# Layer norm over a GNN residual: a zero-filled accumulator, and x added on VectorE

## The reference, cut to what matters

```python
ss = xs[senders]; vv = xv[senders]            # gather
...
msg_s = segment_sum(mid_s, receivers, num_segments=num_nodes)
msg_v = segment_sum(mid_v, receivers, num_segments=num_nodes)
out = concatenate([msg_s @ W_out0 / ..., (msg_v, W_out1) / ...], axis=1) / 16
x = _layernorm(x + out, axis=-1)
```

## Time and profile before

| | |
|---|---|
| time, median of 3 runs | 1347.6 us (1347.39 to 1348.72) |
| the profiled execution: first to last instruction | 1340.7 us |
| outside of that span, median less span | 6.9 us |
| POOL busy | 1046.8 us (78%) |
| PE busy | 977.7 us (73%) |
| DVE busy | 688.6 us (51%) |
| ACT busy | 544.5 us (41%) |

### The profile page before, as it was taken

One profiled execution on the slowest core, in us unless ns is written; L12 is line 12 of the kernel. 1 busy time (PEld: TensorE's weight loads), 2 busy tenths in 40 slices (PEclk: granted clock), 3 DMA queues, 4 the chain that ended last, 5 costly groups with the idle time before them and its releaser, 6 DMA issues.

```text
span 1340.7 us, 26289 instructions
## 1 busy us (share of the span) xinstructions
PE 977.7 (73%) x6206; PEld 919.7 (69%) x6206; DVE 688.6 (51%) x2880; ACT 544.5 (41%) x1403; POOL 1046.8 (78%) x923
## 2 busy tenths in 40 slices
PE   2896777786868868877876777887788778777810
PEld 1795777776767758767776777777777777677710
DVE  5762443466465465465366456366456556545402
ACT  5342232254344434444444435435435444424401
POOL 6547888888888888888888888888888888788771
PEclk9896877878787877887787878787778787878765
DMA  5778853343543443453443443444444444443332
GB/s 154 194 179 189 191 109 62 69 92 41 141 92 41 120 113 41 92 123 59 91 117 67 91 107 75 92 92 90 92 92 90 92 92 91 90 91 67 66 32 64
DMA packets 82531, 130.06 MB, mean 97 GB/s; under 512 B 16168, under 2 KB 66891, under 8 KB 81232
## 3 DMA queue, kind: packets, MB, share of 16 engines
q0 software_dynamic: 68992, 51.43, 28.2%
q1 hardware_dynamic: 12888, 77.14, 17.0%
q10 hardware_dynamic: 632, 1.29, 0.3%
HBM read 78.31 MB, written 77.09 MB: 116 GB/s over the span
## 4 chain that ended last, share of the span: by engine, by line
issue 37%; POOL 28%; DMA 27%; POOLq 6%; SPq 1%; DVE 0%; ACT 0%; ACTq 0%; DVEq 0%
DMA acc<-msg,index_now 17%; POOL sender L444 17%; DMA acc<-in_x_dram 9%; POOL acc L462 8%; POOLq L432 3%; POOL index_now L425 3%; POOLq L433 1%; SPq L297 1%; POOLq L434 0%; POOLq L458 0%; ACT normed L720 0%; DMA total<-acc 0%; POOLq L425 0%; POOLq L461 0%; POOLq L478 0%
## 5 line engine op out<-in xcount | busy, mean ns | idle before, releaser
L462 POOL DMA_INDIRECT acc<-msg,index_now x392 | 624.6, 1593 | 151.9 <-issue 124.9
L444 POOL DMA_INDIRECT sender<-in_x_dram,index_now x392 | 394.1, 1005 | 111.5 <-issue 99.9
L527 PE MATMUL ps_sT<-ident,sender 128*128 128x128 f32 x392 | 83.1, 349 | 269.1 <-DMA sender<-in_x_dram,index_now 268.9
L580 PE MATMUL ps_msg<-outw,sumT 128*128 128x64 f32 x1568 | 254.8, 334 | 0.0
L568 PEld LDWEIGHTS ps_sum<-same,mid 128*128 128x128 f32 x1568 | 248.1, 233 | 9.4 <-DVE mid L960 0.8
L580 PEld LDWEIGHTS ps_msg<-outw,sumT 128*128 128x128 f32 x1568 | 253.6, 253 | 0.0
L527 PEld LDWEIGHTS ps_sT<-ident,sender 128*128 128x128 f32 x392 | 54.7, 174 | 288.6 <-DMA sender<-in_x_dram,index_now 288.5
L568 PE MATMUL ps_sum<-same,mid 128*128 128x128 f32 x1568 | 250.9, 313 | 0.7 <-DVE mid L960 0.7
L938 DVE TENSOR_TENSOR proj<-ps_up,vec_all 128x384 f32<-128x384 f32 x98 | 54.3, 554 | 370.5 <-PE ps_up L548 361.1
L659 ACT COPY sumT<-ps_sum 128x512 f32<-128x512 f32 x196 | 114.9, 586 | 243.6 <-PE ps_sum L568 243.4
L720 ACT ACTIVATE normed<-total,shift,rstd 128x128 f32 x391 | 156.9, 481 | 50.6 <-DVE shift L1011 45.0
(11 more groups left out here) (140 smaller groups left out, 1089.1 us busy)
## 6 DMA issues: line engine op xcount, KB each, us to landing
acc<-in_x_dram SPq DMA_DIRECT2D x80, 312.5 KB
total<-acc SPq DMA_DIRECT2D x30, 832.0 KB
out_dram<-normed SPq DMA_DIRECT2D x29, 832.0 KB
sender<-in_x_dram,index_now POOLq DMA_INDIRECT x392
acc<-msg,index_now POOLq DMA_INDIRECT x392, 3.4
out_dram<-normed ACTq DMA_DIRECT2D x1, 832.0 KB
vec_raw<-in_edge_attr_dram SPq DMA_DIRECT2D x1, 576.0 KB
dst_raw<-in_dst_dram SPq DMA_DIRECT2D x1, 192.0 KB
```

Source lines behind the costliest of these rows:

```text
L444: pool.indirect_dma_start(sender[:, slot, i, :], None, x, bass.IndirectOffsetOnAxis(ap=index_now[:, b, 0, i:i + 1], axis=0)).then_inc(gath ...
L462: pool.indirect_dma_start(acc, bass.IndirectOffsetOnAxis(ap=index_now[:, b, 1, i:i + 1], axis=0), msg[:, msg_slot, i, :], None, compute_op ...
L527: mm = pe.transpose(ps_sT[:, P * i:P * (i + 1)], sender[:, k % RING, i, :], ident[:, :])
L580: mm = pe.matmul(ps_msg[:, i, 2 * MUL * h:2 * MUL * (h + 1)], sumT[:, b, i, h, :], outw[:, h, :], start=True, stop=True)
```

## The change

`acc` is filled with zeros out of SBUF in the same 80 pieces. With each chunk of `acc`, SP also loads the same rows of x into a new buffer `own` (two halves, one for even and one for odd chunks), and VectorE adds them to `total` with one `tensor_tensor` of 128 by 1664 before the `bn_stats`. Both loads count on one semaphore, which the add waits for. The tensor of zeros grows from 384 to 625 columns. The rest of 80 rows is treated alike.

```diff
-        zeros = sb("zeros", [P, SPARE // P, D])
+        zeros = sb("zeros", [P, ZEROS])          # ZEROS = max(PIECE * D, SPARE * D) // P
...
+        own = sb("own", [P, 2, ROWS, D])
...
-                to, of = (a[rows, :].rearrange("n d -> (n d)").rearrange("(p f) -> p f", p=P) for a in (acc, x))
-                sp.dma_start(to, of).then_inc(acc_init[b], 16)
+                to = acc[rows, :].rearrange("n d -> (n d)").rearrange("(p f) -> p f", p=P)
+                sp.dma_start(to, zeros[:, 0:PIECE * D // P]).then_inc(acc_init[b], 16)
...
                 sp.dma_start(total[:, bass.ds(2 * (h % 2) + b, 1), :, :].rearrange("p b r d -> p (b r d)"),
                              acc[bass.ds(N - CHUNK - c * CHUNK, CHUNK), :].rearrange("(p r) d -> p (r d)", p=P)
                              ).then_inc(total_in[b], 16)
+                sp.dma_start(own[:, b, :, :].rearrange("p r d -> p (r d)"),
+                             x[bass.ds(N - CHUNK - c * CHUNK, CHUNK), :].rearrange("(p r) d -> p (r d)", p=P)
+                             ).then_inc(total_in[b], 16)
...
             sp.dma_start(total[0:REST, CHUNKS % 4, 0, :], acc[0:REST, :]).then_inc(total_in[0], 16)
+            sp.dma_start(own[0:REST, 0, 0, :], x[0:REST, :]).then_inc(total_in[0], 16)
...
-            dve.memset(zeros[:, :, :], 0.0).then_inc(zeroed, 1)
+            dve.memset(zeros[:, :], 0.0).then_inc(zeroed, 1)
...
-                dve.wait_ge(total_in[b], 16 * h + 16)
+                dve.wait_ge(total_in[b], 32 * h + 32)
+                both = total[0:parts, quarter, 0:rows, :].rearrange("p b r d -> p (b r) d")
+                dve.tensor_tensor(both, both, own[0:parts, b, 0:rows, :], ALU.add).then_inc(own_added, 1)
+                dve.wait_ge(own_added, c + 1)
+                dve.sem_inc(dve_passed, 1)
```

More of the change, by code:

```diff
@@ L55 @@
 PIECE = 625
+ZEROS = max(PIECE * D, SPARE * D) // P
 PIECES = N // PIECE
@@ L239, in bass_gnn @@
         stat_step = sem("stat_step")
+        own_added = sem("own_added")
+        dve_passed = sem("dve_passed")
         shift_ready = sem("shift_ready")
@@ L286, in _ @@
             sp.wait_ge(zeroed, 1)
-            sp.dma_start(acc[N:N + SPARE, :].rearrange("(p k) d -> p k d", p=P), zeros[:, :, :]).then_inc(spare_rows, 16)
+            sp.dma_start(acc[N:N + SPARE, :].rearrange("(p k) d -> p (k d)", p=P), zeros[:, 0:SPARE * D // P]).then_inc(spare_rows, 16)
             def copy(h, b, waits=True):
```

## The result

| | before | after |
|---|---|---|
| median | 1348.2 us (4 runs, 1347.4 to 1351.1) | 1412.9 us (4 runs, 1411.1 to 1416.2) |
| ratio, 95% interval | | 1.0468 (1.0432 to 1.0503) |
| profiled span | 1340.7 us | 1411.2 us |

The forecast was 1381 us in 1360 to 1398. The direction was right and the added time twice the forecast: 64.8 us by the medians, 70.5 between the two profiled spans. The ratios leave out one execution of the kernel before that was in a slower state, at 1567 us.

A forecast was written before the change was run, and what follows sets the result against it. GpSimd's issue was taken as the bound. Span 1340.7 - 5 (head) + 4 (own's loads) + 30.5 (hold) + 3.9 (tail) = 1374.1, plus 6.9 from span to median: 1381 us, range 1360 to 1398.

The forecast's parts named there:

- The bound: Main loop, 196 to 1246 us: GpSimd's issue sets the time, and everything that waits adds only 11 us.
- The add's hold: Loop: VectorE's 1.88 us add delays GpSimd instructions that start under it, 29 times; +30.5 us, bounds 0 and 51.
- Rival (a): Loop: the add does not hold GpSimd's indirect DMAs at all; 1350.5 us, chance 7%.
- Own's loads: Loop: 29 more loads of 852 KB, hidden from VectorE, slow some scatters; +4 us, bounds 0 and +29.
- rival (c): Loop: scatters caught in three transfers on end land 1 us late per chunk; +29 instead of +4, 1406 us, chance 12%.
- The head: First twelve serial scatters: filling with zeros instead of copying x relieves the DMA engines; -5 us, bounds -19 and +5.
- The tail: After the last scatter: own's load adds 2.0 us and the add 1.88; +3.9 us, bounds +2.5 and +6.
- From span to median: Around the profiled span: the median's 6.9 us above it stays unchanged, taking 1374.1 to 1381 us.
- The range: Whole kernel: 1360 to 1398 us; upper end from hold at 35, loads at 15 and head at -3.

The follow-up runs named there:

- e2: The changed kernel with the add in each chunk, but own loaded only twice in all, so wrong rows are added: 1370.9 us, 1.0194 of the kernel before.
- e5: The changed kernel, complete, with own's load issued some 13 us ahead of the chunk's load: 1375.9 us, 1.0225 of the kernel before.
- e3: The kernel before with acc filled with zeros out of SBUF, nothing of x loaded or added: 1344.3 us, 0.9996 of the kernel before.

## Why the prediction was wrong, step by step

- **The bound.** Right. The loop is set by GpSimd's issue, and what was added shows one for one in it: from the index copy at 195 us, 81 units took 1050.14 us before and 1115.86 after, 65.7 more, of which 28.4 are holds.
- **The add's hold, +30.5 us.** Right, in mechanism and size: 28.4 us held in 29 starts, 29.6 us in the two groups; alone (e2) 22.5 held and 25 to 26 us in time with the tail. (Added up again, the 29 rows of the kernel before give 29.9, not 30.5.) By the Trainium skill (SBUF — State Buffer, Who interferes with whom) two SBUF inputs contend with a GpSimd instruction that reads SBUF; the trace agrees, 0.59 us at 369.07. The same section's inference, that `tensor_tensor` leaves descriptor generation alone, does not hold for indirect DMAs that start under one. Rival (a) is refuted by e2. The forecast price of the add, 1.88 us, was measured as 1.89.
- **Own's loads, +4 us.** This is the step that failed, in one sentence of it above all: "a scatter normally may take until the start of the one after next, 6.4 us, before it delays POOL". The later scatter starts 0.86 us behind the landing, so the room is some 5.5 us. "The greatest landing time is 5.6", "among 392" in rival (c), was wrong too: it was the greatest of 49, and at least 25 in the loop took longer, up to 6.22. So the 0.8 us that I saw between 5.6 and 6.4 wasn't there; two transfers on end had already used the whole room, and cost 5.6 us. With the third on end landings of 7 to 9.2 us stand in the chain, and idle time before scatters grew by 36 us, beyond the +29 that I had as the upper bound. It is rival (c), to which I gave 12%, at 1.2 us a chunk. Its price came from taking one pushed scatter per chunk at 1 us; the waits were up to 3.3. That the place of the third transfer is the cause is shown by e5. Why a burst makes the scatters in it so late isn't shown.
- **The head, -5 us.** Mis-sized: -0.3 between the two profiles, and no change in time in e3. The twelve profiles with zeros have 56.9 to 61.9 us there, the one before 60.3. A cheaper piece only let more pieces come. I had let the engines' share fall from 55 to 43%; it fell to 51. The bound of -19 rested on 3.4 us for a serial scatter, with the same wait behind a landing taken too short.
- **The tail, +3.9 us.** Right: 4.1.
- **From span to median.** 6.9 us were put on top as what lies around the span. The profiled execution of the changed kernel took 1412.9 us with a span of 1411.2, 1.7 apart; the kernel before ran between 1337 and 1356 us over the sessions, and its profile seems to be of a quick execution. Without this the forecast had been 1376.
- **The range.** Its upper end combined a dearer hold with loads at 15 us; (c) together with a hold at its full price, 1406, was left out, and the result lay 7 us above even that.

## What to carry to other kernels

When a queue of small, ordered DMAs sets the pace, look at the slack of their landings before adding bulk traffic, not at the mean load of the engines. Take the slack from a row in which the issuing engine did wait, since the time from landing to the next start (0.86 us here) comes off it, and make sure how many landings a greatest value stands for. Here 256 KB more in a burst were nearly free, 448 KB cost 34 us, and the same 832 KB issued 13 us apart cost nothing. An elementwise operation on VectorE with two SBUF operands is not free beside GpSimd even if VectorE idles half the time: price it as held starts of GpSimd, the add's length less 0.12 us less the start's offset, read off the timeline. Making a filler transfer cheaper does nothing for its neighbours while it is reissued as soon as it lands; pacing it gave 0.8%.

## What the runs showed of the hardware that was not expected

- An indirect DMA that GpSimd starts under a two-input add is held until 0.12 us before the add's end, to within 0.02 us in 114 of 114 cases of three runs; one in e5 that started 0.01 us behind the add's start wasn't held. Under 13 short adds that overlap, 25 of 49 starts were held to the end of the last, one for 1.35 us.
- A scatter that waits for a landing starts 0.81 to 0.97 us behind it, in the loop and in the serial head.
- A scatter of 128 rows landed in 3.2 to 3.4 us alone. The latest one of a burst of a load and a store of 832 KB took 5.5 to 6.2, up to 8.1 with 448 KB more, 9.2 with 832 KB more and 9.7 with 1664 KB more.
- Own's load in rows of 512 bytes instead of 6656 made the scatters no less late.
